# Two pairs of indirect row transfers in flight, and two work orders written anew

## The reference

```python
scores = jax.nn.sigmoid(xf @ gate_w + bias)
top_scores, top_idx = jax.lax.top_k(scores, K)          # K = 2 of E = 8
top_scores = top_scores / (jnp.sum(top_scores, axis=-1, keepdims=True) + 1e-06)
w = jnp.zeros((T, E), dtype=xf.dtype).at[jnp.arange(T)[:, None], top_idx].add(top_scores)
...
combined = jnp.einsum('teh,te->th', eo * 0.1, w)
shared = (jax.nn.gelu(xf @ sw_up + sb_up, approximate=False) @ sw_down + sb_down) * 0.1
out = (shared + combined).reshape(b, s, h)
```

## Time and profile before

| | |
|---|---|
| timed runs | 768.26 us median of 3 (766.97 to 769.05) |
| profiled execution | 762.66 us |
| its span, first to last instruction | 760.9 us |
| TensorE, VectorE, ScalarE, GpSimd busy | 696.3, 505.9, 481.8, 388.6 us |
| mean granted TensorE clock | 0.978 |
| indirect scatters, gathers | 64, 64 |

### The profile page before, as it was taken

How to read it: one execution, slowest core, us unless ns; L and a number is a source line. 1 busy time by engine, 2 the same in 40 slices (tenths; PEclk the granted TensorE clock), 3 DMA queues, 4 the chain that set the end, 5 groups by cost and what they waited for, 6 DMA issues and landing times.

```text
span 760.9 us, 12350 instructions
## 1 busy us (share of the span) xinstructions
PE 696.3 (92%) x3608; PEld 424.0 (56%) x3608; DVE 505.9 (66%) x1906; ACT 481.8 (63%) x734; POOL 388.6 (51%) x562
## 2 busy tenths in 40 slices
PE   4999999999997999887999699996999999999994
PEld 4544444545444544347988699984655544444442
DVE  2598879989998899973452244422345678795572
ACT  2767687677784767565544355552587959777553
POOL 7427354656776667742422255534455575722253
PEclk9999999999999999998999899999899999999998
DMA  9992000000000000028676688811010101000002
GB/s 273 380 383 70 1 1 0 9 15 15 19 19 16 14 15 22 22 84 236 193 203 206 192 249 245 243 51 32 28 29 24 33 23 40 25 4 0 0 15 83
DMA packets 65597, 66.79 MB, mean 88 GB/s; under 512 B 7105, under 2 KB 48410, under 8 KB 65530
## 3 DMA queue, kind: packets, MB, share of 16 engines
q1 hardware_dynamic: 59152, 52.46, 22.8%
q0 software_dynamic: 6320, 13.53, 5.6%
q10 hardware_dynamic: 58, 0.02, 0.0%
HBM read 37.80 MB, written 28.18 MB: 87 GB/s over the span
## 4 chain that ended last, share of the span: by engine, by line
PE 56%; DVE 22%; issue 7%; ACT 5%; DMA 4%; SPq 2%; POOL 2%; DVEq 0%; ACTq 0%; POOLq 0%
PE PS L1085 9%; DVE JK L1271 8%; PE PS L948 4%; PE PS L1135 3%; PE PS L891 3%; PE PS L986 3%; PE PS L1066 3%; PE PS L1149 3%; PE PS L1142 3%; PE PS L897 2%; PE PS L903 2%; PE PS L988 2%; PE PS L911 1%; DMA got<-expert_out,IG 1%; PE PS L1072 1%
## 5 line engine op out<-in xcount | busy, mean ns | idle before, releaser
L1271 DVE CUSTOM_DVE_ANT_0 JK<-PS,CM 128x256 bf16<-128x256 f32 (+1 forms) x512 | 149.1, 351 | 7.0 <-PE PS L948 5.7
L1763 ACT ACTIVATE GF<-PS,XN 128x256 f32<-128x256 f32 x156 | 73.5, 475 | 72.9 <-PE PS L1074 41.6
L948 PE MATMUL PS<-KZ,QS 128*128 128x512 f32 x192 | 88.4, 497 | 7.8 <-DVE MX L1271 5.6
L1085 PE MATMUL PS<-WD,GF 128*128 128x128 f32 x624 | 94.0, 276 | 0.0
L1941 POOL DMA_INDIRECT got<-expert_out,IG x64 | 64.5, 1007 | 50.3 <-DMA got<-expert_out,IG 33.1
L1085 PEld LDWEIGHTS PS<-WD,GF 128*128 128x128 f32 x624 | 86.4, 193 | 2.8
L1913 POOL DMA_INDIRECT expert_rows<-five,IU x64 | 63.3, 990 | 32.5 <-DMA expert_rows<-five,IU 14.9
L1724 ACT ACTIVATE PA<-PS 128x1024 f32<-128x1024 f32 x64 | 64.7, 1026 | 15.2 <-PE PS L971 14.1
L1863 POOL TENSOR_SCALAR H<-xc,MOD 128x256 f32<-128x256 f32 x56 | 33.3, 603 | 68.0 <-DVE xc L1240 60.8
L1900 POOL TENSOR_SCALAR_AFFINE_SELECT PA<-PA 128x256 f32<-128x256 f32 x128 | 49.8, 419 | 27.9 <-ACT PA L1724 27.3
L1924 POOL DMA_DIRECT2D expert_out<-YT x39 | 21.7, 558 | 80.3 <-DVE YT L1523 80.3
(11 more groups left out here) (289 smaller groups left out, 1710.1 us busy)
## 6 DMA issues: line engine op xcount, KB each, us to landing
expert_rows<-five SPq DMA_DIRECT2D x16, 1024.0 KB, 12.6
WU<-in_L_ffn_up_w SPq DMA_DIRECT2D x39, 256.0 KB, 3.2
WD<-in_L_ffn_down_w SPq DMA_DIRECT2D x39, 256.0 KB, 3.4
XT<-expert_rows SPq DMA_DIRECT2D x39, 128.0 KB, 3.7
expert_out<-YT POOLq DMA_DIRECT2D x39, 128.0 KB, 3.4
BD<-in_L_ffn_down_b SPq DMA_DIRECT2D x39, 64.0 KB, 3.3
PA<-in_L_attn_x SPq DMA_DIRECT2D x8, 256.0 KB, 5.5
out<-yo SPq DMA_DIRECT2D x8, 256.0 KB, 2.4
```

Of the source, the lines that this page charges most:

```text
L948: pe.matmul(bk.rearrange("p (j n) -> p j n", n=wd), q, ks, start=True, stop=True).then_inc(sems["mx_mm"], 1)
L1085: m = pe.matmul(bk[:, b], g[:, b], wd[:, k, :], start=(k == 0 and t == 0), stop=(k == 3 and t == blocks - 1))
L1271: m = dve.tensor_tensor_reduce(JK[n % 2][:, s], bk[:, s], CM[:, 256 - wd:256] if wd == 128 else CM[:, 0:256], -1.0, 3.0e38, ALU.add, ALU.m ...
L1763: act.activation(GF[slot["gf", kind, u, k]][:, 0:n], bank("up", kind, u, k)[:, 0:n], ACT.Gelu, bias=bias).then_inc(sems["gelu"], 1)
```

## The change

1. Scatters and gathers: pairs alternate between two semaphores, `scattered[k % 2]` and `gathered[k % 2]`, and a pair waits for the last but one pair before it. Two pairs may be in flight. `cmb`, `hta` and `fetch` now wait for both semaphores; `gathered` has 2 semaphores, not 6, and `got_ready` is gone.
2. The planner has a stage for the landing (`spread`, `got_in`, on an engine "DMA", 2.3 us), a gather is reckoned at 2.3 us instead of 2.35, and two more stages (`atm`, `mxm`) count as narrow for the fillers. The buffer `yo` counts as busy until its store in the planner.
3. ORDER1 and ORDER2 are written anew. Decoded to stage names, ORDER1 gives each engine the same sequence as before. ORDER2 doesn't. On GpSimd it was `gather` of chunk 0 (4), chunk 1 (3), `ln_mod 0`, `gather` 1 3, 2 0, 2 1, `hy 0`; it is now `gather` of chunk 0 (4), chunk 1 (4), 2 0, 2 1, `ln_mod 0`, 2 2, 2 3, `hy 0`. On TensorE `fin2 0` stood behind `up s 4 0` and now stands behind `up s 3 1`, six units (three `up`, three `down`) earlier; `fin2` of the later chunks is mostly earlier too.

```diff
-    "gather": ("POOL", 2.35, None),
+    "spread": ("DMA", 0.0, None), "got_in": ("DMA", 0.0, None), "gather": ("POOL", 2.3, None),
...
-NARROW = {"dpm": 0.06, "rtm": 0.05, "vm": 0.15, "modmm": 0.2}
+NARROW = {"dpm": 0.06, "rtm": 0.05, "vm": 0.15, "modmm": 0.2, "atm": 0.11, "mxm": 0.213}
...
-LANDS = {"gather": 2.5, "scatter": 2.5, "fetch": 3.0}
+LANDS = {"fetch": 3.0, "store": 2.0}
...
         for k in range(4):
-            yield stage("gather", c, k, takes=[] if k else [(GOT, "got", (c,), ("cmb", c))], after=[("gather", c - 1, 3)] if c and not k else [])
-        yield stage("cmb", c, after=[("ev", "s", c)])
+            n = 4 * c + k
+            yield stage("gather", c, k, takes=[] if k else [(GOT, "got", (c,), ("cmb", c))],
+                        after=[("gather", (n - 1) // 4, (n - 1) % 4)] * (n > 0) + [("got_in", (n - 2) // 4, (n - 2) % 4)] * (n > 1))
+        yield stage("cmb", c, after=[("ev", "s", c)] + [("got_in", c, k) for k in range(4)])
...
-            w.wait_ge(*got_ready(c))
+            w.for_all((landed, 64 * (c + 1)) for landed in gathered)
...
-                w.wait_ge(scattered[c % 2], 128 * (c // 2))
+                w.for_all((landed, 64 * (c - 1)) for landed in scattered)
...
-            if k:
-                w.wait_ge(scattered[c % 2], 128 * (c // 2) + 32 * k)
-            elif c:
-                w.wait_ge(scattered[(c - 1) % 2], 128 * ((c - 1) // 2 + 1))
+            if c or k > 1:
+                w.wait_ge(scattered[k % 2], 64 * c + 32 * (k // 2))
             for n in range(2):
...
-                if c:
-                    w.wait_ge(*got_ready(c - 1))
-            else:
-                sem_, all_ = got_ready(c)
-                w.wait_ge(sem_, all_ - 128 + 32 * k)
+            if c or k > 1:
+                w.wait_ge(gathered[k % 2], 64 * c + 32 * (k // 2))
             for n in range(2):
...
-                                        ).then_inc(gathered[b], 16)
+                                        ).then_inc(gathered[k % 2], 16)
...
-            for n in range(2):
-                w.wait_ge(scattered[n], 128 * len(range(n, NCH if t >= N1 else C1, 2)))
+            w.for_all((landed, 64 * (NCH if t >= N1 else C1)) for landed in scattered)
```

More of the change, by code:

```diff
@@ L90 @@
     "t_ev": ("DVE", 0.33, None), "xt": ("PE", 0.218, None), "xs": ("DVE", 0.334, None), "store_rows": ("POOL", 0.55, None),
-    "gather": ("POOL", 2.35, None), "cmb": ("DVE", 2.25, None), "fin1": ("DVE", 1.94, None), "fin2": ("PE", 0.436, None),
+    "spread": ("DMA", 0.0, None), "got_in": ("DMA", 0.0, None), "gather": ("POOL", 2.3, None), "cmb": ("DVE", 2.25, None), "fin1": ("DVE", 1.94, None), "fin2": ("PE", 0.436, None),
     "fin3": ("DVE", 0.784, None), "lc": ("PE", 0.858, None), "ln_sq": ("ACT", 0.48, None), "ln_var": ("PE", 0.858, None),
@@ L133 @@
[L133 to L136, removed]
@@ L429, in dispatch, with lands @@
     def dispatch(c):
-        yield stage("htt", c, takes=[(RR, "ht", (c,), ("ht", c))], after=[("ln_mod", c, "f0")] + ([("scatter", c - 2, k) for k in range(4)] if c > 1 else []))
+        yield stage("htt", c, takes=[(RR, "ht", (c,), ("ht", c))], after=[("ln_mod", c, "f0")] + ([("spread", c - 2, k) for k in range(4)] if c > 1 else []))
         yield stage("hta", c)
         for k in range(4):
-            yield stage("scatter", c, k, after=[("dpd", c)] + ([("scatter", c - 1, 3)] if c and not k else []))
+            n = 4 * c + k
+            yield stage("scatter", c, k, after=[("dpd", c)] + [("scatter", (n - 1) // 4, (n - 1) % 4)] * (n > 0)
+                        + [("spread", (n - 2) // 4, (n - 2) % 4)] * (n > 1))
+    def lands(name, of, c, k):
+        yield stage(name, c, k, after=[(of, c, k)])
     def plan(n):
@@ L443, in fetches @@
         for t in range(n, N1 + NF, NF):
-            yield stage("fetch", t, after=[("woh", NB - 1), ("plan_tiles", int(t >= N1))] + [("scatter", (NCH if t >= N1 else C1) - m, k) for m in (1, 2) for k in range(4)]
+            yield stage("fetch", t, after=[("woh", NB - 1), ("plan_tiles", int(t >= N1))] + [("spread", (NCH if t >= N1 else C1) - m, k) for m in (1, 2) for k in range(4)]
                         + ([("ev", "t", t - NF)] if t >= NF else []))
@@ L502, in schedule @@
                                         weighted(b, 0), weighted(b, 1), divide(b, 0), divide(b, 1), residual(b))]
-        jobs += [(0.0, j) for j in (norm2(c), route(c), count(c), dispatch(c))]
+        jobs += [(0.0, j) for j in (norm2(c), route(c), count(c), dispatch(c), *(lands("spread", "scatter", c, k) for k in range(4)))]
     over = [("woh", b) for b in range(NB)]
@@ L598, in channel @@
         yield stage("om", c, takes=[(BK, "o_bk", (c,), ("yo", c))])
-        yield stage("yo", c, takes=[(YO, "yo", (c,), ("yo", c))])
+        yield stage("yo", c, takes=[(YO, "yo", (c,), ("store", c))])
         yield stage("store", c)
@@ L837, in program @@
     att_done = ("att_x", NB - 1)
-    def got_ready(c):
-        b = slot["got", c]
-        return gathered[b], 128 * sum(slot["got", a] == b for a in range(c + 1))
     def tensor(pe):
```

90 lines of the change are left out of this document (48 added, 42 removed).

## The result

The changed kernel takes 777.57 us (median of 4, 776.15 to 786.59), the kernel before, run beside it, 768.65 (766.97 to 770.64): ratio 1.0123, 95% interval 1.0078 to 1.0168. The forecast was 765.5 (761.1 to 769.9). It was wrong, and in sign.

What follows compares the result with a forecast made beforehand. TensorE was taken to bound the mixer stage's middle, so gains must come from its idle time. -0.15 (wait before `fin2`) and -2.6 (holes) sum to -2.75 us: 768.26 becomes 765.5 us, range 761.1 to 769.9.

Steps and rivals of the forecast that it cites:

- Gathers at a pitch of 1.25 us, no wait for a landing: Mixer start, GpSimd: chunk 0's eight gathers become a chain of issues, the last landing 5.4 us earlier.
- The wait before `fin2` is kept, because six units lie behind it now: Mixer start, TensorE: waits 6.2 us instead of 6.3, low clock behind it kept; net gain 0.15 us.
- rival B: Faster: all 4.8 us of mixer holes go and fillers hold the clock through the wait; -7.15, 761.1 us; chance 0.20.
- Holes in the middle, -2.6 us: Middle of the mixer stage: four TensorE idle holes of 0.89, 0.77, 0.32 and 0.63 us get covered by other work.
- cost and gain nothing: Mixer stage: gathers of the later chunks are ready long before use and don't delay `ln_mod` of chunk 0; 0 us.
- the overlap beyond one pair is free: Mixer start: more than one gather pair in flight costs nothing extra, taken from the 2.55 us landing inside a pair.
- The forecast's rival for a loss: Rival A, at the mixer start: landings over 3.5 us keep gather pairs from overlapping; 770.9 to 773.5 us; chance 0.06.
- C: Slower: ScalarE's three more table changes in the mixer stage, 3.85 us, fall on chunk chains; 769.4 to 772.0 us; chance 0.09.
- D: No change: holes in the mixer stage only change places, within 1.5 us either side; 766.8 to 769.8 us; chance 0.20.
- Rival A: Mixer start: gather pairs don't overlap, period stays 4.06 us, TensorE waits 11.5 before `fin2`; 770.9 to 773.5 us; chance 0.06.
- Scatters 0: Attention and tile stages: GpSimd's 9.1 us of scatter waits go, but the time gains 0, ends 0 and -1.
- Fillers and banks -1 to +0.5: Attention stage: more planner fillers, standing in idle time, change 0 us, with ends -1 and +0.5.

Runs made afterwards that it cites:

- e8: Kernel before with its old orders, two pairs of gathers and scatters in flight, 40 more instructions on VectorE and ScalarE: 0.992 of before.
- e12: Kernel before with its old orders, two pairs of gathers and scatters in flight, each chunk's first gather waiting for the previous chunk's landings: 0.988 of before.
- f3: Changed kernel with each chunk's first gather waiting for the previous chunk's landings, run beside f1 on one chip: 0.996 of before.
- e5: Changed kernel with 40 more wait instructions at the head of VectorE's and ScalarE's programs: 770.3 us, 1.006 of before.
- f1: The changed kernel itself, measured again on one chip with f2 and f3: 1.011 of before.
- e4: Changed kernel with its orders, fillers and banks, but one pair of gathers and one pair of scatters in flight: 785.7 us, 1.025 of before.
- e2: Kernel before with two pairs of gathers and two of scatters in flight, its own orders, fillers and banks: 764.0 us, 0.997 of before.
- e1: Kernel before with two pairs of gathers in flight; its orders, fillers, banks and scatters stay: 766.7 us, 0.998 of before.
- e6: Changed kernel with each chunk's first gather waiting until all gathers of the chunk before have landed: 764.0 us, 0.998 of before.
- f2: Changed kernel with 40 more instructions on VectorE and ScalarE (e5 again), run beside f1 on one chip: 1.027 of before.
- g1: e7 once more, on another chip: changed kernel with an unread fill on GpSimd behind each of the first ten gather pairs: 1.008 of before.
- e7: Changed kernel with GpSimd filling a tile nobody reads behind each of the first ten gather pairs: 772.7 us, 1.007 of before.
- e3: Changed kernel with each pair of gathers waiting for the pair before it, two pairs of scatters still in flight: 787.2 us, 1.028 of before.

## Why the prediction was wrong

*Gathers at a pitch of 1.25 us, no wait for a landing.* Right. All 20 came so, and the first combination began 11.3 us after the first gather (527.57 - 516.23), as worked out (522.5 - 511.14 = 11.4); it was 16.8.

*The wait before `fin2` is kept, because six units lie behind it now.* Right, 5.70 us where the text has 6.2, with the low clock behind it (1.91 us for a `down`), so the 2.2 us of rival B did not come. e8 and e12 give the price of that choice of the order. There the old order meets the short gathers, and TensorE hardly waits and keeps its clock (e12):

```profile
531.01 0.66 PE L1094 MATMUL PS<-CT,on 128*128 128x128 f32 x4 [0.34 <-DVE on L1556]
```

Mixer stage 242.0 against 246.7 with the new order and the same drain (e12, f3), 241.4 against 246.3 without hold-ups (e8, e5): 4.7 to 4.9 us for the six units that I put at 5.25. The gain of the gathers is all there; the new order doesn't take it.

*Holes in the middle, -2.6 us.* Right in sum. e5, the new order without hold-ups, has 246.3 us where before has 249.8: -3.5, and the sum said -2.75. The variance of chunk 0 waits 0.37 us instead of 1.13 and the 0.61 of chunk 1 is gone; 0.63 us new stand before a later `lc`.

*That the later gathers "cost and gain nothing", and that the overlap beyond one pair is free because it is free inside a pair.* This is the step that failed. I priced the overlap by the landing of the transfers and by the wait that GpSimd has for them. In a run without gaps TensorE's updates came up to 15.2 us late, and ScalarE and VectorE, and behind them TensorE, waited for that: 258.2 - 246.3 = 11.9 us of mixer stage between after and e5, 12.6 between f1 and f3. Take 11.9 from the measured +8.4 and -3.5 is left. The forecast's rival for a loss looked for longer landings (over 3.5 us) and sat on the wrong engine. No row of before could have told it: the updates in that profile are all on time.

*Rivals B, C and D.* Without hold-ups the mixer stage came out where the forecast had it, so none of them is needed. The three more table loads of C are there (43 against 40 from the first gather on) and e5 shows no loss from them.

*Rival A (the pairs don't overlap: 770.9 to 773.5).* e4 is that rival built, with the fillers of the change: 785.7. TensorE waits 9.88 us before `fin2` where the rival has 11.5, so that part was sized well enough. What it lacks is that the ten pairs ahead of `ln_mod` delay it once a pair takes 4.06 us and not 2.5: 6.36 us before the variance, where 1.13 stood, and 2.21 at a later one.

*Scatters 0.* Right as far as it was measured: the attention stage isn't longer or shorter for them (246.8 us in e2 and 247.3 in e1).

*Fillers and banks -1 to +0.5.* This term was sized wrong too. The fillers came as feared by the planner, 18 instead of the 10 of the earlier trace rows:

```profile
L855 PE MATMUL PS<-CT 128*128 128x128 f32 x18 | 3.5, 296 | 0.0
```

Their cost isn't the 2 us of matmuls. In the profiles of e6, f2 and g1 the granted clock is low for 13.7 us from near 197 us on, and the attention stage takes some 256 us; in the others it takes 243 to 249. Windows from 195 to 210 us of e7 and of g1, the same kernel:

```profile
195.00:210.00 15.00, 14.36 (x85) 6.78 (x85) 14.66 (x87) 12.35 (x17) 11.19 (x20) 1.00 0.06 19
```

```profile
195.00:210.00 15.00, 15.00 (x57) 5.78 (x58) 10.43 (x55) 9.68 (x13) 7.59 (x12) 0.54 0.02 5
```

The clock is at its upper level, 2.4 GHz, in the first and near the lower, 1.2 GHz, in the second; TensorE was busy throughout either way. With the change's orders, fillers and banks 32 of 77 executions had a mean clock of 0.963 or less, with those of before 3 of 132. So the planner's output does cost something in the attention stage: in about four executions of ten, and within one kernel these are 6 to 11 us longer than its others (e5, e6, e7, f3). I expected 0.5 at most. Which of the three, fillers, banks or the later order, brings it wasn't tried.

*The end.* No change, as said: 1.12 us before L1161 and before L1182 where 0.56 and 1.02 stood.

## What to carry to other kernels

Price an overlap by what all engines do during it, not by the waits of the engine that issues: here GpSimd's queue got faster and TensorE's word to two others came late. Where an engine idles and the profile names no releaser, look for the update of the semaphore that it waits for: it tells a late signal from a stopped engine. Keep runs of indirect transfers short (eight here) with a gap behind each; it costs 2.5 us of an engine that doesn't bound and gave back 12 where there were hold-ups (nothing where there were none: e5 and e6, both 246.3). And measure the enabling change with the order unchanged first: the wait counts, the old orders and the drain make the kernel 1.2 to 1.9% faster than before (0.988 and 0.981), while the same with the new orders is 0.996.

## What the hardware showed that was not expected

During an unbroken run of indirect DMA issues on GpSimd (0.94 us each, 0.30 between), TensorE's semaphore updates came up to 15.2 us behind the ends of their matmuls, and ScalarE and VectorE, which waited for them, were idle up to 14.8 and 12.4 us. In all twenty traces every update that is over 0.3 us late is TensorE's; none of VectorE's, ScalarE's or GpSimd's is. Whether TensorE's results were late as well can't be told, since the ends of matmuls are modelled; its next matmuls began on time (533.12 and 534.82 in after). In the nine profiles that have a hold-up in a run of 14 or 20, VectorE went on between 0.3 us before and 3.6 us after the run's last issue, ScalarE between 6.6 us before and 2.6 us after it. VectorE had worked inside the run for 4.6 us (`cmb` and `fin1`) before it stood, at its usual durations, and TensorE took its release from VectorE in 0.06 us meanwhile. The Trainium skill, page SBUF — State Buffer, section Who interferes with whom, knows one contention between compute engines, the port pair that VectorE and GpSimd share. It doesn't fit: ScalarE, which isn't part of it, stood longest, and what was late came from TensorE.

The late updates come and go between groups of runs. Runs of 14 or 20 gathers have hold-ups in all nine profiles of the first measurement and three groups, in neither of the two of another group (e5, e8). On one chip they are there in one group and not in the next. They go with traces that lack semaphore updates, and the recording itself is not excluded as their cause. What decides it, and what keeps TensorE's updates back, stays open. That in such a group the run of issues brings them is shown by f1 against f3 on one chip, and by their absence in the mixer stage of e3 and e4.
